# The FFN input of each batch: turned by SBUF-to-SBUF DMAs and VectorE block transpositions in place of TensorE transpositions, with new order tables

## What is computed

```python
x = x + layernorm(attention(layernorm(x)))      # 8 x 512 x 512
h = layernorm(x)                                # the FFN input
scores = sigmoid(h @ router_weight.T)           # 16 experts, two chosen for each token
routed = sum over the two chosen experts of weight * (relu(h @ w_up[e])**2 @ w_down[e])
shared = relu(h @ shared_up)**2 @ shared_down
x = x + layernorm(routed + shared)
```

## Time and profile before

| | us |
|---|---|
| median of three runs | 1635.28 (1633.22 to 1638.73) |
| the profiled execution: its own time | 1637.92 |
| its span, first to last instruction | 1636.1 |
| attention, from 0 to about | 905 |
| first list, about 905 to 1116, and no matmul until | 1138 |
| experts, 1138 to about | 1429 |
| combine, 1429 to the end | 1636.1 |

### The profile page before, as it was taken

The page is one execution under the profiler, slowest core; times in us unless marked ns, Lnnn a source line. Parts: engine busy times, 40 slices in busy tenths (PEclk is TensorE's granted clock), DMA queues, the critical chain, the costliest instruction groups (busy, mean ns, idle before and its releaser), DMA issues.

```text
span 1636.1 us, 21814 instructions
## 1 busy us (share of the span) xinstructions
PE 1518.9 (93%) x7006; PEld 1028.9 (63%) x7006; DVE 970.2 (59%) x1871; ACT 783.9 (48%) x1417; POOL 797.5 (49%) x820
## 2 busy tenths in 40 slices
PE   4799999999999999999998998894999999979997
PEld 3465656656556566565653776683666666657886
DVE  3566767676766667676666426831333333339998
ACT  2355566565665656656547452330222222255554
POOL 1177696776957778769678410002222222133341
PEclk9799999999999999999999999897999999989999
DMA  4757368475583764737842234207977777596773
GB/s 117 207 134 215 85 187 259 114 206 148 152 247 103 218 194 129 222 107 203 278 130 79 77 134 157 90 20 222 296 219 218 216 212 211 169 332 216 232 238 127
DMA packets 169415, 291.32 MB, mean 178 GB/s; under 512 B 20596, under 2 KB 72692, under 8 KB 163156
## 3 DMA queue, kind: packets, MB, share of 16 engines
q1 hardware_dynamic: 150280, 242.21, 48.9%
q0 software_dynamic: 12912, 41.82, 8.7%
q10 hardware_dynamic: 6112, 5.90, 1.2%
HBM read 154.07 MB, written 92.01 MB: 150 GB/s over the span
## 4 chain that ended last, share of the span: by engine, by line
PE 75%; DMA 8%; DVE 6%; SPq 4%; issue 3%; ACT 3%; POOL 2%; DVEq 0%; POOLq 0%; ACTq 0%
PE bank L113 13%; PE bank L729 9%; PE bank L775 8%; PE bank L798 8%; PE bank L707 7%; PE bank L628 6%; PE bank L614 6%; PE bank L633 5%; PE bank L644 5%; DMA a<-kq_scratch 4%; PE bank L653 2%; SPq L1753 2%; DMA kq_scratch<-a 1%; PE bank L787 1%; POOL a L1594 1%
## 5 line engine op out<-in xcount | busy, mean ns | idle before, releaser
L1594 POOL TENSOR_TENSOR a<-a 128x512 f32<-128x512 f32 x384 | 497.2, 1325 | 121.6 <-PE bank L653 65.0
L1404 ACT ACTIVATE a<-bank 128x512 f32<-128x512 f32 x512 | 298.0, 598 | 250.1 <-PE bank L633 216.6
L908 DVE TENSOR_REDUCE a<-bank 128x1 f32<-128x512 f32 x512 | 323.6, 680 | 65.3 <-PE bank L614 64.5
L113 PE MATMUL bank<-a 128*128 128x512 f32 (+1 forms) x864 | 238.8, 400 | 5.9 <-DVE a L854 4.0
L628 PE MATMUL bank<-a 128*128 128x512 f32 x512 | 222.6, 435 | 4.9 <-ACT a L1404 4.1
L614 PE MATMUL bank<-a 128*128 128x512 f32 x512 | 185.1, 430 | 25.6 <-DMA a<-kq_scratch 21.5
L633 PE MATMUL bank<-a 68*128 68x512 f32 x512 | 206.6, 403 | 1.1 <-ACT a L1394 0.2
L707 PE MATMUL bank<-c 128*128 128x512 f32 x768 | 185.8, 403 | 19.4 <-ACT c L1477 7.4
L113 PEld LDWEIGHTS bank<-a 128*128 128x128 f32 (+1 forms) x864 | 160.3, 188 | 48.2 <-issue 4.4
L707 PEld LDWEIGHTS bank<-c 128*128 128x128 f32 x768 | 148.8, 195 | 55.3 <-issue 8.8
L1663 POOL DMA_INDIRECT f<-h_scratch,f x79 | 74.9, 949 | 217.0 <-DMA f<-f 214.5
(11 more groups left out here) (185 smaller groups left out, 1753.7 us busy)
## 6 DMA issues: line engine op xcount, KB each, us to landing
a<-kq_scratch SPq DMA_DIRECT2D x192, 256.0 KB, 5.9
kq_scratch<-a SPq DMA_DIRECT2D x32, 1024.0 KB, 4.1
a<-a SPq DMA_DIRECT2D x80, 256.0 KB, 5.4
f<-f SPq DMA_DIRECT2D x316, 64.0 KB
yp_scratch<-f SPq DMA_DIRECT2D x79, 256.0 KB, 3.2
a<-in_L_attn_x SPq DMA_DIRECT2D x15, 1024.0 KB, 9.1
x_scratch<-a SPq DMA_DIRECT2D x8, 1024.0 KB, 7.2
h_scratch<-a SPq DMA_DIRECT2D x8, 1024.0 KB, 13.0
```

The costliest lines, as they stand in the source:

```text
L113: t = e.matmul(out, a[n], b[n], start=n == 0 and m == 0, stop=n == len(ah) - 1 and m == 2)
L908: e.tensor_reduce(K.mx[:, i, j:j + 1], K.MX[n % 3][:], AX.X, ALU.max).then_inc(Z.max, 1)
L1404: e.activation(K.pt[:, n % NP, :], K.SC[n % 2][:], ACT.Exp, scale=SCALE).then_inc(Z.exp, 1)
L1594: e.tensor_tensor(K.acc[:, j, :], a, K.pt[:, n % NP, :], ALU.add).then_inc(Z.acc, 1)
```

## The change

`turn2` leaves TensorE and ScalarE. In its place stand four `move h` and four `turn2`, one for each 128 tokens. `move h` issues four DMAs of 64 KB from `yb` to `xb` (which has been stored by then): the features 128q to 128q+127 of 128 tokens go to the partitions 32q to 32q+31. In batches 0 to 6 SP issues all sixteen, in batch 7 ScalarE issues eight of them. `turn2` is one VectorE transposition of 32x32 blocks of 128x512 elements from `xb` to `hs`; its first waits for all sixteen DMAs. `route` on TensorE waits for the four transpositions. The features then stand in another order over the partitions, so the router weights and the shared expert's first weights are permuted before the launch. The helper `turn_rows` holds the four DMAs. Two semaphores fall away, which others take over. All numbers of `STEP` and `FIRST_STEP` are new.

```diff
 def after_order(b):
     return ([("project", b, i) for i in range(4)], norm_order("y", b), norm_order("h", b),
-            [("turn2", b, k) for k in range(4)] + [("route", b), ("fold", b)])
+            [("move h", b, i) for i in range(4)], [("turn2", b, i) for i in range(4)] + [("route", b), ("fold", b)])
...
-        "r2": 10, "v3": (13, 14, 19, 20), "turn23": (0, 4, 17, 21), "route3": 27, "fold3": 30, "project0": (18, 23, 23, 34),
+        "r2": 10, "v3": (15, 15, 19, 20), "move3": (0, 0, 0, 0), "turn23": (12, 16, 17, 28), "route3": 26, "fold3": 31,
...
         if b:
-            put("turn2", [("turn2", b - 1, k) for k in range(4)])
+            put("move", [("move h", b - 1, i) for i in range(4)])
+            put("turn2", [("turn2", b - 1, i) for i in range(4)])
...
+def turn_rows(e, out, rows, sem):
+    for q in range(4):
+        e.dma_start(out[HD * q:HD * q + HD, :], rows[:, q * P:(q + 1) * P]).then_inc(sem, 16)
...
-    def turn2(b, k):
-        bank = begin("turn2", b, k)
-        for i in range(4):
-            w.wait_ge(Z.scaled["h"], 4 * b + i + 1)
-            t = e.transpose(bank[:, i * P:(i + 1) * P], K.yb[:, i, k * P:(k + 1) * P], K.ident[:])
-        t.then_inc(*end("turn2", b, k))
...
         w.wait_ge(Z.w3, 4 * 16)
+        w.wait_ge(Z.hT2, 4 * (b + 1))
         for k in range(4):
-            drained("turn2", b, k)
...
+    def turn2(b, i):
+        w.wait_ge(Z.hm, 16 * 16 * (b + 1))
...
+        e.transpose(K.hs[:, :, i * P:(i + 1) * P].rearrange("p k (r i) -> p k i r", i=4),
+                    K.xb[:, i, :].rearrange("p (i k c) -> p k i c", k=4, c=HD)).then_inc(Z.hT2, 1)
...
-        e.copy(K.hs[:, k, :], bank[:]).then_inc(*end("turn2", b, k))
+    def move_h(b, i):
+        if b == B - 1 and i % 2:
+            w.wait_ge(Z.x1s, 16 * (b + 1))
+            w.wait_ge(Z.scaled["h"], 4 * b + i + 1)
+            turn_rows(e, K.xb[:, i, :], K.yb[:, i, :], Z.hm)
...
+    def move_h(b, i):
+        if b < B - 1 or i % 2 == 0:
+            w.wait_ge(Z.x1s, 16 * (b + 1))
+            w.wait_ge(Z.scaled["h"], 4 * b + i + 1)
+            turn_rows(e, K.xb[:, i, :], K.yb[:, i, :], Z.hm)
...
+    given["L0_ffn_shared_up"] = np.ascontiguousarray(given["L0_ffn_shared_up"].reshape(4, 4, HD, SI).swapaxes(0, 1).reshape(D, SI))
```

More of the change, by code:

```diff
@@ L146 @@
 FIRST_STEP = {
[L147 to L152, removed]
[11 rows of a table removed]
+        "rest": (1, 1, 1, 1, 1, 1, 2, 2, 2, 4, 4, 6, 7, 7, 5, 6, 8, 8, 3, 6, 8, 8, 8, 8, 9, 9, 9, 10, 8, 9, 9, 10, 11, 11, 11, 11, 12, 13),
+        "prepare": (18,),
+        "early": (13, 14, 14, 14, 15, 16, 16, 16, 17, 17, 17, 19, 19, 19, 19, 20, 20, 20, 21, 21, 28, 30, 36, 37, 37, 38),
+        "late": (22, 22, 23, 23, 23, 23, 23, 23, 23, 23, 23, 23, 24, 24, 24, 25, 25, 25, 25, 25, 25, 26, 26, 26, 26, 26, 30, 30, 30, 31, 32, 32, 33, 33),
+        "weights": (31, 35, 39), "invert": (33, 33, 34, 34, 44, 45, 45, 45, 56)}
+STEP = {"split up": (10, 20, 25, 29, 31, 32, 38, 43), "split h": (32, 34, 35, 41), "last values0": 8, "total0": 9, "invert0": 9,
[11 rows of a table added]
 def beside_order(u):
@@ L345, in combine_order @@
     return out + settle() + settle()
-FILLS = ("turn", "proj", "half", "rows", "v", "total", "project", "turn2", "route", "fold", "bias")
+FILLS = ("turn", "proj", "half", "rows", "v", "total", "project", "route", "fold", "bias")
 class Sems:
@@ L361, in __init__ @@
         self.x2, self.x1s, self.h2s, self.hTs = make("x2_in"), make("x1_out"), make("h_out"), make("hT_out")
+        self.hm, self.hT2 = make("h_moved"), make("hT_done")
         self.full, self.free = many("ms_full", 2), many("ms_free", 2)
@@ L384, in __init__ @@
             "hTt_done", "eu_full", "e_relu", "e_square", "eT2_full", "eaT_done", "ed_full", "yo_done"))
-        self.su2, self.sd2 = many("su2_in", 4), make("sd2_in")
+        self.su2 = many("su2_in", 4)
         self.su2_hi, self.sd2_hi = make("su2_high"), make("sd2_high")
@@ L932, in project @@
             w.wait_ge(Z.h2s, 16 * b)
-            m = K.fill["turn2", b - 1, 3]
-            w.wait_ge(Z.full[m % 2], m // 2 + 1)
-        e.tensor_tensor(K.yb[:, i, :], bank[:], K.bo[:], ALU.add).then_inc(*end("project", b, i))
+            w.wait_ge(Z.hm, 16 * 16 * b)
+        e.tensor_tensor(K.yb[:, i, :], bank[:], K.bo[:], ALU.add).then_inc(*end("project", b, i))
+    def turn2(b, i):
+        w.wait_ge(Z.hm, 16 * 16 * (b + 1))
+        if b:
+            m = K.fill["route", b - 1]
+            w.wait_ge(Z.full[m % 2], m // 2 + 1)
+            w.wait_ge(Z.hTs, 16 * b)
+        if b + 2 < B:
+            m = K.fill["proj", b + 2, "r"]
+            w.wait_ge(Z.full[m % 2], m // 2 + 1)
+        e.transpose(K.hs[:, :, i * P:(i + 1) * P].rearrange("p k (r i) -> p k i r", i=4),
+                    K.xb[:, i, :].rearrange("p (i k c) -> p k i c", k=4, c=HD)).then_inc(Z.hT2, 1)
     def fold(b):
@@ L1157, in place @@
         chained()
-        e.tensor_tensor(flat(a), flat(a), K.TR[0][:], ALU.add).then_inc(Z.prefix, 1)
+        e.tensor_tensor(flat(a), flat(a), K.TR[0][:], ALU.add).then_inc(*choice.next())
         yield
-        w.wait_ge(Z.prefix, 1)
+        chained()
         for oh, sl in ((K.oh1, K.sl1), (K.oh2, K.sl2)):
@@ L1672, in gather @@
         elif n >= 4:
-            w.wait_ge(Z.sd2, 16)
+            w.wait_ge(Z.sd, 2 * 16)
         else:
@@ L1772, in scale, with turn2 @@
             e.dma_start(hv[b], K.yb[:]).then_inc(Z.h2s, 16)
-    def turn2(b, k):
-        if k == 3:
-            for i in range(4):
-                drained("turn2", b, i)
+    def move_h(b, i):
[3 more added lines that the diff above has]
+            turn_rows(e, K.xb[:, i, :], K.yb[:, i, :], Z.hm)
+    def turn2(b, i):
+        if i == 3:
+            w.wait_ge(Z.hT2, 4 * (b + 1))
             e.dma_start(K.hT_d[b], K.hs[:]).then_inc(Z.hTs, 16)
@@ L1826, in move @@
             w.wait_ge(Z.hTt, i - 3)
-        for q in range(4):
-            e.dma_start(K.hx[HD * q:HD * q + HD, n, :], K.ht[:, n, q * P:(q + 1) * P]).then_inc(Z.hx[n], 16)
+        turn_rows(e, K.hx[:, n, :], K.ht[:, n, :], Z.hx[n])
     def e_down(i):
@@ L1889, in finish @@
         e.dma_start(K.outv[t], K.x1[:, z, :]).then_inc(Z.cs[z], 16)
-    stages = {"load": load, "proj": proj, "qr": qr, "send": send, "again": again, "residual": residual, "scale": scale, "turn2": turn2, "early su": early_su,
+    stages = {"load": load, "proj": proj, "qr": qr, "send": send, "again": again, "residual": residual, "scale": scale, "move h": move_h, "turn2": turn2, "early su": early_su,
               "early hT": early_hT, "load sd": load_sd, "split h": split_h, "weights": weights, "prepare": prepare, "move": move, "e down": e_down,
```

24 lines of the change are left out of this document (9 added, 15 removed), and 20 rows, old and new, of the table STEP.

## The result

The changed kernel takes 1644.20 us (median of seven runs, 1641.18 to 1648.17) against 1635.28 (seven runs, 1633.22 to 1638.73). The ratio is 1.0052 with a 95% interval of 1.0035 to 1.0069: slower by 6 to 11 us, where the likeliest case was 8 us faster. The profiled execution took 1644.6 us with a span of 1642.8 (before: 1637.92 and 1636.1), so this pair shows 6.7 us of the 8.9 between the medians: the profiled execution of the kernel before lies 2.6 above its median, that of the changed kernel 0.4.

A forecast was written before the change was run, and what follows sets the result against it. It took TensorE's queue to bound attention, with GpSimd bounding the last unit. Attention +6.6 and first list with hole -15.2 gave -8.6 us from the median 1635.28, about 1627, range 1608 to 1646.

The forecast's parts named there:

- What bounds the kernel: Attention: TensorE's queue is the path, 103.2 of 105.4 us a batch; the last unit is under GpSimd.
- The stack wait: Fourth unit's opening: TensorE has 1.8 us less work and waits 1.8 longer, leaving 0.6 of 2.4 us a batch, -3.6 us.
- The first list's slow stretch: Behind the 7.38 us wait, 24 matmuls run some 2.8 us too long; both go, -10.2 us.
- The price of the moves: SP's queue in attention: sixteen moves take 3.6 us a batch, between 0 and 6.7; SP itself delays send under 1 us.
- the second rival: Moves take longer, each batch's wait grows: attention 6(t - 1.9) - 3.6, 1650 us at t = 7.5; batch above 108; chance 0.20.
- The qr wait of 10.2 us: Next unit's first score step: qr, delayed behind the moves, makes TensorE wait 1.7 us a batch, 10.2 in six.
- VectorE covered: Attention: VectorE, busy 73 of 105 us, has room for transpositions of 0.707 us, 2.8 a batch; its waiting adds nothing.
- Attention in sum: Six batches: -3.6 from the turn leaving TensorE plus 10.2 of qr waits, +6.6 us.
- First list and hole: Up to the experts: +1.5 at totals, -10.2 behind it, -6.5 in the hole; -15.2 us, between -3 and -21.
- the tail of batch 7: First list up to totals: turn leaves TensorE but route waits for moves; +1.5 us, between -4.0 and +6.
- the queue does not swallow the moves: Rival on SP's queue: idle time takes up the moves with no new wait, -18.8, 1616 us; chance 0.20.
- the hole does not keep its length: Rival on the hole before the experts: it keeps most of its length, first list gives 4, 1638 us; chance 0.12.

The follow-up runs named there:

- e7: The changed kernel with its moves left out in attention and the first list, so the turned h is another; 1629.3 us.
- e9: e7 with k3 and q3 at 0, so both half of the fourth unit stand ahead of the stack; 1612.2 us.
- e6: e3 with both half ahead of the maxima (k3, q3 at 0) and the moves kept ahead of send (move3 at -1); 1644.3 us.
- e10: e6 with qr3 at 0 instead of 27: SP issues the next batch's qr behind the moves and ahead of send; 1645.3 us.
- e1: The changed kernel with the attention table of the kernel before, only move3 and turn23 taken from the new table; 1650.8 us.
- e3: The changed kernel with the four VectorE transpositions at 24 to 27 of the fourth unit, behind the maxima, and route3 at 29; 1641.0 us.
- e4: The changed kernel with k3 and q3 at 0: both half ahead of the stack, which also put send ahead of the moves; 1722.8 us.
- e8: The kernel before with only the changed kernel's FIRST_STEP (without the four entries for move h), turn on TensorE; 1621.3 us, ratio 0.9934.
- e5: e1 with the four VectorE transpositions at 24 to 27 of the fourth unit and route3 at 29; 1656.2 us, ratio 1.0139.
- e11: e8 with q3 at 0 instead of 4: the second half of the fourth unit ahead of the maxima; 1614.2 us, ratio 0.9885.

## Why the prediction was wrong, step by step

- **What bounds the kernel**: right. The chain from `proj r` to the first maxima takes 15.9 us before and 14.8 after (234.2 to 249.06); it does not shrink by as much as TensorE's work in it, which becomes waiting. The stack wait was forecast at 3 us and is 3.00; over six units it went from 9.4 to 18.5 us, +9.1 where 10.8 were put down.
- **What the wait sets off**: left out, and this is the step that failed in attention. The sum took each wait at its length. Behind five of the six stack waits TensorE is at 1.2 GHz; in six batches that time goes from 10.2 to 23.9 us, 6.9 us of work lost where nothing was put down. The trace of the kernel before had the sign in other batches than the one that was read. Behind a stack wait of 2.67 us three maxima take 1.51 us there instead of 0.97; from the timeline before:

```profile
458.09 1.51 PE L614 MATMUL bank<-a 128*128 128x512 f32 x3 [2.67 <-DMA a<-kq_scratch]
```

The first list's slow stretch was priced; the same was not asked of the fourth unit. e7 has this step without the moves: -3.6 by the forecast, +2.8 measured, with the same 23.9 us at 1.2 GHz. e9 fills the opening, and 16.6 us go.
- **The price of the moves**: the size came out near, by another way than the one named, so by luck. 10.2 us were put down in six batches for what stands behind them, all as a wait for qr; e7 measures 9.4, and no such wait is there. The time in the queue was mis-sized: 3.6 us a batch were taken between 0 and 6.7, and the trace shows 5.3, past the 5.0 above which the second rival is slower than before. That rival's formula gives 6(5.3 - 1.9) - 3.6 = +16.8 in attention and +1.6 in all. A batch takes 649.6 / 6 = 108.3 us, above the 108 that were named as its mark, but the cost goes through VectorE (below) and not through qr. SP needed 15.0 us for the issues, not 9.7 (0.60 to 1.67 each), and `send` went out at 259.55 instead of 250.04, where SP was to delay it by under 1 us. The Trainium skill ("DMA: Bandwidth & Descriptors", section on queues, rings and completion order) says that descriptors are consumed in ring order on each DMA engine; the first move agrees, which lands 12.4 us after its issue at 244.44 and so with the h store. The 0.95 us that the same page of the Trainium skill gives (section on bandwidth) are for one 64 KB transfer from HBM issued by GpSimd; they are no price for sixteen in a row, which took 0.33 us each here.
- **The qr wait of 10.2 us**: not in the changed kernel, and there all the same. qr lands 6.7 us after its last issue, at 267.89 + 6.7 = 274.6, and TensorE, late by its other waits, comes at 276.17. In e6, where it is on time, L640 waits 2.0 to 3.0 us. The mechanism exists, but the wait overlaps with the others and does not add to them: e10 takes it away and the six batches are only 1.8 us shorter.
- **VectorE covered**: wrong. The wait for the moves is 1.53 us, the transposition 1.09 us instead of 0.707, 4.4 us a batch instead of 2.8, and the reductions stand behind them. Counted waits of the maxima for VectorE go from 2.9 to 6.5 us in six batches; the rest falls by 7.7 us where 14.4 of work left, so another 6.7 are put down to waits too short to count (3.8 of them go with the moves, by the rest of e7). Together that is 10.3 us where nothing was put down, about as much as the qr wait that did not come. That VectorE's transpositions can hold up the maxima is shown by e1, e3 and e4.
- **Attention in sum**: work and short waits -7.7, idle time +13.0, clock +6.9: +12.2 where +6.6 was forecast. VectorE's waits and the missing qr wait cancel; the clock does not.
- **First list and hole**: right in sign and mechanism, -12.2 for -15.2; the term that was mis-sized is the tail of batch 7. The hole came to 12.43 (forecast 14) with 1.5 us of new wait ahead (1.6); `totals` waits 1.01 instead of 3.98, and the 7.38 us are gone. The tail of batch 7 was put at +1.5: by e8 the new turn costs 4.8 us there, and by e7 its moves alone 5.2, among it `route`'s 1.41 and the 2.06 for ScalarE's copy behind four issues of moves. The 2.28 in front of them is not the turn's, it stands in e8 as well (2.30). Without the new turn the table gives 17.0.
- **In all**: -8.6 was forecast and the profiled pair shows +6.7. Of the 15 us between them 5.6 lie in attention's six batches, 3.0 in the first list, and 6.6 in the three stretches for which 0 was put down, with no cause shown.
- **The other rivals**: the queue does not swallow the moves (e7: 9.4 us in the six batches), and the hole does not keep its length.

## What to carry to other kernels

Work that stands in front of a late transfer gains nothing when it is taken away: fill that place again in the same change (e9 against e7: 1.4 us of work, 2.8 us a batch). Price a wait on TensorE with the slow clock behind it, and price transfers by all that stands behind them in the queue and on the engine that waits for them. Read the wait that a change will lengthen in every batch, not in one. Where a change comes with new tables, measure the tables alone: the gain here was the first list's, and e8 has it without the new turn.

## What the runs showed of the hardware

A 128x512 fp32 transposition of 32x32 blocks takes 1.09 us when its output has a stride of four elements (L945) and 0.71 when its output runs in blocks of 32 neighbouring elements (L1234). Sixteen DMAs of 64 KB behind a 1 MB store land 0.33 us apart, while SP takes 0.65 us for each issue in e4 (10.45 / 16) and 0.94 in the changed kernel (15.00 / 16). A wait of 2.02 us for VectorE in the midst of full work was followed by 1.2 GHz (e5), while e11 with waits under 1 us stayed at 2.4 GHz through six batches. In between the length alone does not tell: in the kernel before a stack wait of 1.38 us (at 775.58) was followed by matmuls at 1.2 GHz, and in e9 one of 2.31 us (at 662.55) was not.
